# A masked linear layer with a gated LoRA mixture on one core: the written step orders of all five engines replaced, 44 idle transposes ahead of the first product

## What is computed

```python
def reference(...):
    xn = _layernorm(x)
    bm = mask.reshape(32, 32, 32, 32).sum(axis=(1, 3)) > 0
    s = einsum('bsk,nk->bsn', xn, weight * bm) + bias
    base = einsum('bsi,oi->bso', xn, W_org)
    q = einsum('bi,ki->bk', xn.mean(axis=1), Wq)
    coeffs = softmax(einsum('bk,ek->be', q, lora_keys) / sqrt(128))
    h = einsum('bsi,eir->bser', xn, lora_down)
    delta = einsum('be,bser,ero->bso', coeffs, h, lora_up)
    return x + s * silu(base + delta)
```

## Time and profile before

| what | value |
|---|---|
| median of 3 runs | 432.62 us (431.58 to 432.65) |
| profiled execution, first to last instruction | 437.0 us (no time of its own is recorded beside it) |
| PE busy | 417.0 us (95%) |
| DVE, ACT, POOL busy | 384.2, 241.2, 54.3 us |
| DMA | 110.51 MB, mean 253 GB/s |
| mean granted PE clock | 0.988 of 2.4 GHz |

### The profile page before, as it was taken

The page is one execution under the profiler, slowest core; times in us unless marked ns, Lnnn a source line. Parts: engine busy times, 40 slices in busy tenths (PEclk is TensorE's granted clock), DMA queues, the critical chain, the costliest instruction groups (busy, mean ns, idle before and its releaser), DMA issues. The chain is left out here.

```text
span 437.0 us, 6104 instructions
## 1 busy us (share of the span) xinstructions
PE 417.0 (95%) x1857; PEld 336.3 (77%) x1857; DVE 384.2 (88%) x592; ACT 241.2 (55%) x427; POOL 54.3 (12%) x61
## 2 busy tenths in 40 slices
...
PEclk9699999999999999999999999999999899999999
...
GB/s 304 400 397 174 142 150 301 303 220 301 270 272 284 326 202 255 353 352 333 325 302 199 95 74 244 174 375 348 315 366 336 271 44 177 59 241 230 170 232 200
DMA packets 46176, 110.51 MB, mean 253 GB/s; under 512 B 4800, under 2 KB 7104, under 8 KB 45376
## 3 DMA queue, kind: packets, MB, share of 16 engines
...
...
## 5 line engine op out<-in xcount | busy, mean ns | idle before, releaser
L1005 PE MATMUL psA<-b_hi,a_hi 128*128 128x512 f32 (+1 forms) x444 | 173.9, 392 | 1.4 <-ACT snaps L1273 0.9
L1007 PE MATMUL psA<-b_hi,a_lo 128*128 128x512 f32 (+1 forms) x444 | 172.1, 388 | 0.0
L1006 PE MATMUL psA<-b_lo,a_hi 128*128 128x512 f32 (+1 forms) x444 | 172.0, 387 | 0.0
L1005 PEld LDWEIGHTS psA<-b_hi,a_hi 128*128 128x128 f32 x444 | 83.4, 188 | 21.1 <-ACT snaps L1273 2.2
L1007 PEld LDWEIGHTS psA<-b_hi,a_lo 128*128 128x128 f32 x444 | 83.4, 188 | 17.3
L1006 PEld LDWEIGHTS psA<-b_lo,a_hi 128*128 128x128 f32 x444 | 83.4, 188 | 16.3
L1388 DVE TENSOR_TENSOR b_lo<-b_raw,b_hi 128x512 fp32r<-128x512 f32 (+2 forms) x78 | 59.7, 790 | 0.0
L1229 ACT ACTIVATE b_hi<-b_raw 128x512 fp32r<-128x512 f32 (+2 forms) x66 | 44.8, 717 | 21.7 <-DVE b_raw L1395 7.8
L1273 ACT ACTIVATE snaps<-psA 128x512 f32<-128x512 f32 x39 | 23.0, 590 | 35.2 <-PE psA L1007 35.2
L1215 ACT ACTIVATE a_hi<-s_raw 128x512 fp32r<-128x512 f32 x52 | 31.7, 623 | 15.6 <-DVE s_raw L1379 13.9
L1388 DVE TENSOR_TENSOR a_lo<-s_raw,a_hi 128x512 fp32r<-128x512 f32 x52 | 35.1, 688 | 1.0 <-ACT a_hi L1215 0.8
...
## 6 DMA issues: line engine op xcount, KB each, us to landing
...
```

Of the source, the lines that this page charges most:

```text
L1005: nc.tensor.matmul(ps, l_hi, r_hi, start=first, stop=False, skip_group_check=True)
L1006: nc.tensor.matmul(ps, l_hi, r_lo, start=False, stop=False, skip_group_check=True)
L1007: return nc.tensor.matmul(ps, l_lo, r_hi, start=False, stop=over, skip_group_check=True)
```

## The change

All five strings of `ORDER` are rewritten. The steps of SP, ACT, DVE and POOL are the same steps, each on the same engine as before, in another order (292, 377, 546 and 40 of them). PE's 200 steps are kept too, and two are added, `F0.30` and `F1.14`, which run 30 and 14 transposes of the identity into the bank of the warm-up. The products keep their order among each other.

```diff
 ORDER = (
     """
-    LX0 LX2 LM0 LX1 LX3 LW0.0 LW0.1 LM1 LX4 LW1.1 LW1.0 LM2 LM3 LI LW2.0 LK LY LX5 RS2 LW3.0 ST2 RS0 LX6 LX8 RS1 RS4
...
+    LX0 LX2 LX1 LM0 LM1 LW0.0 LW0.1 LX3 LW1.1 LW1.0 LM2 LX4 LW2.0 LM3 LI LY LK RS0 RS1 LW3.0 RS3 LX5 LX6 LX8 ST3 ST2
...
     """
-    TX0.0 TX0.1 CP0 P0 TX1.0 TX1.1 CP1 TX2.0 TX2.1 P1 P2 CP2 TX3.0 P3 TX3.1 K P4 CP3 TX4.0 P5 TX4.1 P6 P7 P8 P9 P10
...
+    TX0.0 TX0.1 F0.30 CP0 F1.14 CP1 TX2.0 P0 TX1.0 TX1.1 TX2.1 P1 P2 CP2 TX3.0 P3 P4 TX3.1 P5 K CP3 P6 TX4.0 TX4.1 P7
...
     """
-    TC0.0 CA0.0 TC0.1 H4 H6 HB0.0.2 CA1.1 CA1.0 TC1.0 H2 H0 TC1.1 HB0.0.0 HB0.0.3 HB0.1.0 CA2.1 CA2.0 TC2.0 TC2.1
...
+    TC0.0 CA0.0 CA1.0 CA1.1 HB0.0.0 TC0.1 H4 HB0.0.1 H0 HB0.0.2 H6 TC1.0 HB0.0.3 H2 HB0.1.1 TC2.1 CA2.1 CA2.0 TC1.1
...
@@
             for st in pe_steps:
                 kind = st[0]
-                if kind == "CP":
+                if kind == "F":
+                    for _ in range(st[2]):
+                        nc.tensor.matmul(psA[:, ACC - 1, 0:P], ident[:, :], ident[:, :], start=True, stop=True,
+                                         is_transpose=True)
+                elif kind == "CP":
```

More of the change, by code:

```diff
@@ new lines @@
+    LE0.2.1 LD0.2.1 LE0.3.0 LD0.3.2 ST57 LE0.3.1 LD0.2.2 ST56 LE0.2.3 LE0.3.3 LE0.3.2 LE0.2.2 LD0.2.3 LD0.3.3 ST55 ST58
+    RS15 LG9.0 LG9.1 LB1 LR0 LR2 LB3 LB0 LB2 LG10.0 LG10.1 LR1 LB4 LR3 LR4 ST60 LG11.0 ST66 ST64 LB5 LG11.1 LR6 ST65
+    LB6 LB7 LR7 ST67 LR5 LR8 LG12.0 LB8 ST70 LR9 LB10 LG12.1 ST72 LR10 LB12 LB9 LR11 LB11 ST74 LR12 ST73 LU1.1.1 LR13
+    LU1.1.0 LU1.7.0 ST77 LU1.7.1 LB14 LU1.3.0 LB13 ST79 LD1.1.0 LU1.3.1 LD1.1.3 LU1.2.0 LD1.0.0 LD1.0.3 LU1.2.1 ST80
+    LB15 LD1.0.1 LR14 LD1.1.1 LR15 LE1.0.0 LE1.1.0 LD1.0.2 LD1.1.2 LE1.0.1 LE1.1.1 LE1.0.3 LE1.1.3 LD1.2.0 LE1.0.2
@@ new lines @@
+    LE1.1.2 LD1.3.0 LD1.2.1 LE1.2.0 LE1.2.1 LE1.3.0 LD1.3.1 LD1.2.2 LE1.3.1 LD1.2.3 LD1.3.2 LE1.2.3 LE1.2.2 LE1.3.3
+    LE1.3.2 LB16 LD1.3.3 LB18 ST84 ST83 LG13.0 LB19 LG14.0 ST86 LB17 LG13.1 LR16 LG14.1 LR17 LR18 ST85 LG15.0 LR19 LB21
+    LR20 ST92 ST88 LB20 LG15.1 LR21 LR22 LB22 ST93 LR23 ST94 LB23 LR24 ST98 LB25 ST95 LB27 LB24 LR25 LB26 ST100 ST101
+    ST102 LR27 LR26 LR29 LB30 LR28 LR30 LB28 LB31 LB29 ST105 ST108 ST107 LR31 ST111 ST112 ST113 TS0 TS1
+    """,
+    """
+    TX0.0 TX0.1 F0.30 CP0 F1.14 CP1 TX2.0 P0 TX1.0 TX1.1 TX2.1 P1 P2 CP2 TX3.0 P3 P4 TX3.1 P5 K CP3 P6 TX4.0 TX4.1 P7
@@ L188 @@
[L188 to L193 removed]
+    E0.3.3 P59 P60 P61 P62 P63 P64 P65 P66 P67 P68 P69 P70 P71 P72 P73 P74 P75 P76 P77 P78 P79 P80 P81 P82 P83 P84 P85
```

115 lines of the change are left out of this document (60 added, 55 removed).

## The result

The changed kernel takes **439.53 us** (median of 4 runs, 438.28 to 442.02) against 432.63 (431.58 to 432.71) for the kernel before on the same chip: ratio 1.0176, 95% interval 1.014 to 1.0213. It is slower by 1.8%, 7 us. The prediction said 429.4 and its range ended at 433.9.

A forecast was written before the change was run, and what follows sets the result against it. PE, busy 95% of the span, was taken as the bound. -1.2 - 4.0 - 1.9 - 0.8 + 0.5 = -7.4 gave 429.6 from the span; the timed median without the 4.0 gave 429.2; forecast 429.4, range 425.2 to 433.9.

The forecast's parts named there:

- the two new orders of ACT and DVE: Between 23 and 226 us PE hardly idles, so these orders gain nothing and may cost; +0.5 us.
- the start: Up to P0: later weights cost 1.3 us, idle transposes keep P0 at full clock; gain 1.2 us.
- the E stages: PE's three stops near 228, 313 and 338 us shrink or go through reordered loads; -6.7 us.
- all or nothing: At P0: clock stays up and P0 takes 3.6 us instead of 6.06, or it drops and the start loses.
- its worst end of +1.3: At the start: if the clock drops in the idle time before CP1, up to 1.3 us lost.
- Place 338: PE's stop near 338 us and its half clock: load LD1.2.1 goes out six microseconds earlier; -4.0 of 4.35 us.
- place 228: PE's stop near 228 us: load LE0.3.1 issued earlier ends DVE's wait for its worg tile; -1.9 us.
- place 313: PE's stop near 313 us: load LD1.1.0 goes ahead of two others; -0.8 of 1.2 us.
- the sum of the timed runs: Whole kernel from the timed median, without the stop at 338: 432.6 - 1.2 - 1.9 - 0.8 + 0.5 = 429.2.
- Slower: Rival at the start: P0 late behind mask 1's count, clock falls, 1.9 us lost, no E-stage gains; 434.5 us, 15%.
- The rule on transposes and the clock: Rival at P0: transposes don't engage the upper clock, so P0 runs at half rate; 2.5 us more, 431.9; 9% with its variant.

The follow-up runs named there:

- a_v54: Changed kernel with DVE's pair of a_lo splits ahead of mask 3's copy and the bank-freeing copy QC2 moved earlier; 436.61 us, ratio 1.0111.
- before, again: The kernel before, unchanged, run for a second profile; 433.18 us, span 431.3.
- b_sp3: The kernel before with only three loads of the E stages issued earlier; 431.33 us, ratio 0.997.
- The two edits: DVE's a_lo pair and QC2 moved earlier (a_v54), then one group-9 sum moved from POOL to DVE as well (a_s92); together 435.32 us.
- a_s92: a_v54 with one sum of group 9 also moved from POOL to DVE; 435.32 us, ratio 1.0073.
- a_p0: Changed kernel with P0 put back ahead of CP1 on PE and 30 idle transposes ahead of it instead of 14; 442.6 us, ratio 1.0229.

## Why the prediction was wrong
The prediction forecast -7.4 us and +7 came. Three of its terms failed: the two new orders of ACT and DVE, put at +0.5, cost 6.6 us in the profile; the start, put at -1.2, cost 2.2; and the E stages, put at -6.7, gave some 1.4.

**Start.** P0 was put at 17.1 and came at 17.48. The number is near and the reason was not: not the two counts of mask 1 were last (over at 14.6, forecast 16.1) but DVE's `bmx`, behind its masking of W0.1 and shut out by POOL for 0.85 us. The transposes took 3.44 and 1.73 us, within their bounds, yet CP0 came at 11.58 instead of 12.3, so they were over at 13.4 and the hole was 3.1 us, not 2.2. The clock fell in after's profiled run: P0 gained 0.1 us, not 2.5; in a_v54's it stayed, behind a hole just as long (3.60 us), so the forecast's all or nothing was itself the wrong form. The start was forecast at -1.2 us; at 47 us after was 2.2 behind, more than its worst end of +1.3. Of the difference 0.4 are P0's later start and 0.7 that P0 ends earlier in before, again (20.59) than in the profile that the prediction read (21.26).

**Place 338, -4.0, place 228, -1.9, place 313, -0.8.** The mechanism held: moved alone, the loads remove the stops. The size was read from one run that had more of them than the others. The 7.5 us are 3.6 in the second profile, and the timed runs gave 1.3 (b_sp3) for what the sum of the timed runs priced at 2.7. That I left out the stop at 338 but kept the two others in full was the fault in this step. In after the three stops are gone and two other loads stop PE instead. One is LD1.3.0, which the prediction had at most 0.4 us late: DVE's add EG1.1.1, put at 323, began its pair at 330.67, of which only 4.9 us are PE's own lag behind that profile, so LD1.3.0 and LD1.2.1 went out at 332.44, and E1.3.1 waited 0.86 us. Against the profile that the prediction read the three places gave back 1.0, 0.9 and 3.6 us net of the new stops, 5.5 of the 6.7; against before, again they gave 1.4, and behind the second stage, between 355 and 370 us, as much is lost again.

**"The new ACT and DVE orders gain nothing and may cost", +0.5.** This is the term that failed most. It was sized by PE's small stops of before, and what came was one stop of 2.04 us with 1.6 us of half clock behind it at 50, and 2.7 us around 250 to 280. Both have the same cause: an order that puts two-input DVE operations beside POOL's. The view to read was not PE's but DVE's and POOL's timelines at POOL's few long operations; the prediction never looked at what now stands beside them. The two edits that take the consequences out return 4.2 of the 7 us or so (1.0176 to 1.0073 in the ratio). The other 3 us I can place only in part. In the profiles they are 2.1 us of lag of PE behind before, again, that grows from 0.9 us at 47 to 2.0 at 113 and is 2.1 at the end. The 0.9 is P0's, which ends at 22.17 there against 20.59, less the 0.65 us moved ahead of it; a late `snaps` of ACT at 112 (0.49 us) is in the rest.

One cause was left untested. The two edits moved what stands behind two collisions; they took almost none away. DVE is still busy for 396.9 us in a_s92 against 385.1 in before, again, with one step of 0.7 us more, and some fifteen of its operations still stand long beside POOL's, where some five do in before, again. One of them:

```profile
21.50 3.00 DVE L1390 TENSOR_TENSOR b_lo<-b_raw,b_hi 128x512 fp32r<-128x512 f32 x2
```

Two such splits take 1.28 us elsewhere. No run takes these out, so how much of the 3 us is theirs, and which steps they pass it on through, remains open. a_p0 shows only that putting P0 back ahead of CP1 does not win it back.

**The rivals.** "Slower" had the start nearly right (P0 past 17.15 at half clock, its price 1.9 us, measured 2.2) and ended at 434.5, since it, too, knew nothing of the collisions. The rule on transposes and the clock ("TensorE: Matmul & The Clock Gate", Part 4, in the Trainium skill) was rightly doubted: with 30 and 16 transposes and no hole P0 took 4.01 us at 1.00. What they did not secure is the clock over a hole of 2.4 to 3.1 us behind them.
